# A three-layer transformer on one core: the order of four groups of TensorE work, one moved DMA, and score matmuls of half the width

## The reference

```python
def layer(x, c, w):                      # x: (16, 256, 288), c: (16, 288)
    m0, m1, m2, m3, m4, m5 = split(silu(c) @ w.ada + b_ada, 6)
    q, k, v = heads((layer_norm(x) * (1 + m1) + m0) @ w.qkv + b_qkv)
    attn = softmax(q @ k.T / sqrt(18))   # per sequence and head, 256 x 256
    x = x + m2 * ((attn @ v) @ w.out + b_out)
    h = gelu((layer_norm(x) * (1 + m4) + m3) @ w.up + b_up)
    return x + m5 * (h @ w.down + b_down)
```

## Time and profile before

| | |
|---|---|
| median of 3 runs | 2386.28 us (2383.67 to 2392.12) |
| profiled execution | 2383.67 us, its span 2381.7 us |
| PE busy | 2171.7 us, 91% of the span |
| PEld busy | 1880.9 us, 79% |
| DVE busy | 1382.9 us, 58% |
| ACT busy | 1055.5 us, 44% |
| POOL busy | 993.1 us, 42% |

### The profile page before, as it was taken

The page is one execution under the profiler, slowest core; times in us unless marked ns, Lnnn a source line. Parts: engine busy times, 40 slices in busy tenths (PEclk is TensorE's granted clock), DMA queues, the critical chain, the costliest instruction groups (busy, mean ns, idle before and its releaser), DMA issues. The chain is left out here.

```text
span 2381.7 us, 51475 instructions
## 1 busy us (share of the span) xinstructions
PE 2171.7 (91%) x16443; PEld 1880.9 (79%) x16443; DVE 1382.9 (58%) x3142; ACT 1055.5 (44%) x1859; POOL 993.1 (42%) x988
## 2 busy tenths in 40 slices
PE   6988874789999999898999999998989999999996
PEld 2767653688888888787888888887878888988886
DVE  5378625465656565765656565657556565656551
ACT  2011121445454545454454545453544545454542
POOL 0000002454545454456545454544565454545444
PEclk9755696899999999999999999999999999999998
DMA  8000042433332323234332323332442333332320
GB/s 200 10 2 0 25 150 81 118 95 96 82 99 80 100 78 102 78 106 127 90 101 78 102 81 99 85 98 72 117 118 74 97 85 98 87 97 83 97 72 23
DMA packets 139306, 207.42 MB, mean 87 GB/s; under 512 B 35771, under 2 KB 95835, under 8 KB 138919
## 3 DMA queue, kind: packets, MB, share of 16 engines
q1 hardware_dynamic: 111576, 164.00, 25.3%
q10 hardware_dynamic: 24192, 27.94, 4.3%
q0 software_dynamic: 3456, 14.43, 2.1%
HBM read 99.74 MB, written 20.82 MB: 51 GB/s over the span
## 5 line engine op out<-in xcount | busy, mean ns | idle before, releaser
L1679 DVE TENSOR_REDUCE maxima<-scores 128x4 f32<-128x1024 f32 x384 | 452.4, 1220 | 189.2 <-PE scores L1434 188.6
L1022 POOL TENSOR_TENSOR hidden<-g_full,hidden 128x512 fp32r<-128x512 f32 (+1 forms) x240 | 280.9, 1188 | 347.9 <-ACT hidden L1256 347.6
L1213 ACT ACTIVATE probs<-scores 128x1024 f32<-128x1024 f32 x384 | 383.2, 1026 | 72.9 <-PE pv_ps L1471 47.2
L1496 PEld LDWEIGHTS mlp_ps<-h_mlp,w_up 128*128 128x128 f32 (+1 forms) x3024 | 363.9, 191 | 59.8 <-ACT hidden L1256 34.0
L1496 PE MATMUL mlp_ps<-h_mlp,w_up 128*128 128x256 f32 (+1 forms) x3024 | 384.7, 285 | 28.6 <-ACT hidden L1256 23.2
L1352 PE MATMUL mlp_ps<-w_down,hidden 128*128 128x288 f32 x2592 | 392.0, 296 | 0.0
L1352 PEld LDWEIGHTS mlp_ps<-w_down,hidden 128*128 128x128 f32 x2592 | 373.0, 190 | 21.1
L1434 PE MATMUL scores<-k_stack,q_stack 108*128 108x512 f32 x768 | 252.3, 422 | 40.0 <-DVE maxima L1679 24.0
L1203 ACT ACTIVATE neg_max<-att_ps 16x256 fp32r<-16x256 f32 x48 | 18.0, 374 | 530.3 <-PE att_ps L1444 530.3
L1457 PE MATMUL scores<-q_stack,k_stack 110*128 110x256 f32 x1536 | 246.1, 292 | 4.5 <-ACT probs L1213 3.2
L1457 PEld LDWEIGHTS scores<-q_stack,k_stack 110*128 110x128 f32 x1536 | 206.2, 189 | 34.3 <-issue 19.8
(11 more groups left out here) (171 smaller groups left out, 3412.6 us busy)
## 6 DMA issues: line engine op xcount, KB each, us to landing
q_stack<-qk SPq DMA_DIRECT2D x144, 180.0 KB
k_stack<-qk SPq DMA_DIRECT2D x288, 90.0 KB
inv_sum<-inv_scratch ACTq DMA_DIRECT2D x192, 128.0 KB, 2.8
k_stack<-qk SPq DMA_DIRECT2D x288, 54.0 KB
x_in<-out_x SPq DMA_DIRECT2D x48, 288.0 KB, 3.9
x_mid<-out_x SPq DMA_DIRECT2D x48, 288.0 KB, 4.2
out_x<-x_out SPq DMA_DIRECT2D x48, 288.0 KB, 3.1
q_stack<-qk SPq DMA_DIRECT2D x144, 72.0 KB
```

The costliest lines, as they stand in the source:

```text
L1022: tt(out, full, high.bitcast(F32), ALU.subtract).then_inc(signal, 1)
L1213: evict(probs[:, u % 4, :, :, :], scores[u % 2][:, :, :, :], ACT.Exp, scale=SCALE)\
L1496: last = mm(up_bank[n % 2][:, (m % 2) * T:(m % 2 + 1) * T], w[:, m * P:(m + 1) * P], h, start=count == 0, stop=count == 6)
L1679: nc.vector.tensor_reduce(out=maxima[:, :, :, u], in_=scores[u % 2][:, :, :, :], axis=AX.X, op=ALU.max).then_inc(s_max, 1)
```

## The change

- `negated_maxima`, `negate_maxima`: both DMAs of negated maxima are now sent by SyncE, one after the other; ScalarE sends none and no longer waits for its own eviction.
- `score_unit`: a unit's scores are made by four matmuls of 256 columns (head outside, query tile inside), each with its own weight load, where there were two of 512. The output's index order changes with it, and `unit_max` writes its four results with the two indices exchanged.
- `half_step` of TensorE: `weighted_values` 0 moves ahead of the MLP transposes and of shifted unit 4; shifted unit 5 moves ahead of `weighted_values` 1; `up` 1 moves behind `values` 1, and on ScalarE `gelu` 1 moves behind `v_evict` 1.
- In the score phase each part of `down` comes ahead of its score unit.

```diff
--- before.py
+++ after.py
@@ -956,10 +956,11 @@
                         head_into_stack(j, par, K_PARTS[j], slice(2, 5), 2 * PAIR + HD * par, slice(5, 8), s_stack_b)
 
             def negated_maxima(it):
-
                 hold(s_neg, it + 1 + PRE)
-                sp.dma_start(q_stack[PAIR_ROWS:PAIR_ROWS + 1, :, :].bitcast(F32),
-                             neg_max[0:H // 2, :].bitcast(F32)).then_inc(s_neg_st, 16)
+                for par in range(2):
+                    row = PAIR_ROWS + par
+                    sp.dma_start(q_stack[row:row + 1, :, :].bitcast(F32),
+                                 neg_max[par * 8:par * 8 + 8, :].bitcast(F32)).then_inc(s_neg_st, 16)
 
             def store(it, b):
                 hold(s_x_out, 2 * it + 2 + PRE2)
@@ -1201,9 +1202,6 @@
                 act.wait_ge(s_max_ps, it + 1 + PRE)
                 act.wait_ge(s_neg_st, 32 * it + 16)
                 evict(neg_max[:, :], att_ps[0:H, 0:T], ACT.Copy, scale=-1.0).then_inc(s_neg, 1)
-                act.wait_ge(s_neg, it + 1 + PRE)
-                act.dma_start(q_stack[PAIR_ROWS + 1:PAIR_ROWS + 2, :, :].bitcast(F32),
-                              neg_max[H // 2:H, :].bitcast(F32)).then_inc(s_neg_st, 16)
 
             def exponentials(it, u):
                 act.wait_ge(s_st, 8 * it + u + 1 + PRE)
@@ -1302,12 +1300,10 @@
                     load_table(ACT.Gelu_apprx_tanh)
                     gelu(it - 1, 0)
                 load_sums(it)
-                if before:
-                    gelu(it - 1, 1)
                 if after:
                     v_evict(it + 1, 1)
                 if before:
-                    for n in range(2, UP_USES):
+                    for n in range(1, UP_USES):
                         gelu(it - 1, n)
                         if n == 2:
                             store_inverse(it)
@@ -1430,9 +1426,10 @@
                 else:
                     pe.wait_ge(s_max, 8 * it + u - 1)
                 r = slice(0, PAIR_ROWS)
-                for qt in range(2):
-                    last = mm(scores[u % 2][:, qt, :, :], q_stack[r, u, qt * P:(qt + 1) * P],
-                              k_stack[r, u, :, :], start=True, stop=True)
+                for par in range(2):
+                    for qt in range(2):
+                        last = mm(scores[u % 2][:, par, qt, :], q_stack[r, u, qt * P:(qt + 1) * P],
+                                  k_stack[r, u, par, :], start=True, stop=True)
                 last.then_inc(s_score, 1)
 
             def maxima_transposes(it, after):
@@ -1543,12 +1540,12 @@
                         qk_tiles(it + 1, n, m_between=before)
                     shifted_unit(it, n)
                 shifted_unit(it, 3)
+                weighted_values(it, 0)
                 if before:
                     mlp_transposes(it - 1, after)
                 shifted_unit(it, 4)
-                weighted_values(it, 0)
+                shifted_unit(it, 5)
                 weighted_values(it, 1)
-                shifted_unit(it, 5)
                 shifted_unit(it, 6)
                 if after:
                     values(it + 1, 0)
@@ -1561,11 +1558,10 @@
                     if at(b, 1):
                         pe.wait_ge(s_w_low, converted(OF["w_up"][2], l))
                     up(m, 0)
-                    up(m, 1)
                 if after:
                     values(it + 1, 1)
                 if before:
-                    for n in range(2, UP_USES):
+                    for n in range(1, UP_USES):
                         if at(b, 1) and n == 2:
                             weights_ready("w_up", l)
                         up(m, n)
@@ -1577,10 +1573,10 @@
                 if at(b, 1):
                     weights_ready("w_down", l)
                 for n in range(6):
+                    if before:
+                        down(m, n // 3, n % 3)
                     if after:
                         score_unit(it + 1, n + 2)
-                    if before:
-                        down(m, n // 3, n % 3)
 
             def epilogue():
                 it = L * B - 1
@@ -1676,7 +1672,7 @@
                 if u == 0:
 
                     dve.wait_ge(s_max_ps, it + PRE)
-                nc.vector.tensor_reduce(out=maxima[:, :, :, u], in_=scores[u % 2][:, :, :, :],
+                nc.vector.tensor_reduce(out=maxima[:, :, :, u].rearrange("p q r -> p r q"), in_=scores[u % 2][:, :, :, :],
                                         axis=AX.X, op=ALU.max).then_inc(s_max, 1)
 
             def inverse(it):
```

## The result

The changed kernel takes 2419.38 us (median of 4 runs, 2416.54 to 2432.57), against 2389.2 us for the kernel before in 4 runs of the same session (2383.67 to 2401.7). The ratio is 1.0134, with a 95% interval of 1.0101 to 1.0167. It is slower by 1.3%, clear of 1 by its interval, as forecast; 2421 was predicted. The profiled execution took 2419.03 us, its span 2417.1.

What follows compares the result with a forecast made beforehand. TensorE is 91% busy, but VectorE's chain was taken to set the half step's end; terms 0.3 - 0.3 + 0.13 + 0.65 + 0.03 = +0.8 us, times 38 = 30.4, plus 4.8 for odd ones, gave 2421 us (range 2388 to 2440).

Steps and rivals of the forecast that it cites:

- The forecast's case: Whole program: slower, 2421 us, with VectorE setting the end of the half step; chance 0.77.
- VectorE's chain: Score phase: score unit 2, maximum 2, `normalise`, GpSimd 5.4 us, the `attention_high` cast, maxima 6 and 7, then transposes.
- D: Score phase, `down` ahead of score units: unit 2 0.96 us later, maximum 2 and `normalise` 0.65 later; +0.65 us.
- plain half step: 38 of 47 intervals between maxima transposes, alike, 39.25 us in the one read; predicted +0.8 us each, 30.4 in all.
- A: Both negated-maxima DMAs on SyncE: the second lands late for shifted unit 0; +0.3 us, bounds 0.1 and 0.6.
- B: Weighted values 0 and shifted unit 5 moved earlier: exponential 7 starts sooner, a gain of 0.3 us, bounds 0 and 0.53.
- C: `values` 1 ahead of `up` 1: new wait of some 0.3 us, `up` 2 loses its wait; net +0.13.
- E: Score matmuls of 256 columns instead of 512: extra weight loads hide; +0.03 us, bounds 0 and 0.1.
- rival 3: Score units: added weight loads are exposed, 3.2 us per half step, so 2536 us; chance 0.03.
- odd half steps: The 9 intervals between maxima transposes that are not plain, estimated without rows; together +4.8 us.
- Rival 1: Score phase: TensorE is the bound and VectorE's lateness is hidden; faster, -0.5 us per half step, 2367 us; chance 0.12.
- Rival 2: Whole program: no change, the DMA move hidden and `down` first half hidden; 2386 us; chance 0.08.

## Why the prediction was right, and where it was not

The forecast's case held: VectorE's chain sets the end of the half step, and D makes it longer. Its signs came too: 4.07 us from the first maximum to `normalise` (about 4.1 forecast); `values` 1 waits for `v_sb`, 1227.34 - 1225.39 - 1.69 = 0.26 us; weighted values 2 and 3 together take 1225.39 - 1223.20 = 2.19 us instead of the 1.87 of two groups without a wait, so 0.32 is left of the 0.53. TensorE's idle time at the end is 0.92 us, a little under the 1 us named. The terms, in us per plain half step:

| part | predicted | alone | in the changed kernel |
|---|---|---|---|
| A | +0.3 (0.1 to 0.6) | +0.25 | |
| B | -0.3 (-0.53 to 0) | +0.18 | -0.29 (not run: 0.74 less the other four alone) |
| C | +0.13 (-0.15 to +0.4) | +0.09 | |
| D | +0.65 (0 to 0.95) | +0.66 | +0.21 (undone) |
| E | +0.03 (0 to 0.1) | +0.03 | |
| sum | +0.81 | +1.21 | +0.74 |

The last column's entries for B and D do not add up with each other: B's counts D at its full 0.66, D's is what its removal gives back.

- **A** was read well. The second DMA is issued at about 1209.94 + 0.70 = 1210.64 and shifted unit 0 starts at 1212.67, so issue to use is 2.0 us: the nearer bound, of the earlier trace rows, and not the 2.31 of the earlier trace rows (by which the second DMA would be 1150.68 + 0.70 + 2.31 - 1153.25 = 0.44 us late, not the 0.47 of the text). The restart of the stream adds 0.1. The Trainium skill (DMA: Bandwidth & Descriptors, Issuing engines are not separate DMA queues) says that issuing from several engines saves only the sequencer's time, which is usually small beside the transfer. The trace agrees about what is saved, 0.70 us of issuing. Here that was enough to become a wait in 45 half steps.
- **B** gave 0.37 us at `up` 0 when alone, a little more than the 0.3 taken. In the changed kernel the gain cancels A's 0.27 up to `up` 0. Its cost was missing from the sum: shifted unit 4 releases SyncE's copies, and their last six come 1.2 us later (0.7 to 0.9 with B alone). I named this in the last sentence as a surprise and did not price it. The trace before had the rows for it: unit 5 needs copies whose issue ends at 1174.94 + 4.91 = 1179.85, and it starts at 1149.70 + 32.26 = 1181.96. In the changed kernel the price is zero only because D delays unit 5 by 0.95 us. So the -0.3 came true by D's doing, and with D undone it would not have.
- **C** made its wait of 0.3; the net was 0.08 to 0.09 instead of 0.13.
- **D** was right to 0.01 us as an edit of the kernel before, and so was its path: unit 2, maximum 2, `normalise`, GpSimd, the cast, maxima 6 and 7. The Trainium skill (SBUF — State Buffer, section on the two separate sides) has the later of VectorE and GpSimd blocked for the whole of the other's instruction. The traces agree: the cast ends 0.15 us behind GpSimd's low parts, and in the two runs that only moved it away from them 1.18 and 1.40 us became 0.28.
- **E** was nothing to speak of. The rule on row groups that the prediction cites from the Trainium skill (TensorE: Matmul & The Clock Gate, section The mechanism) does not hold for these matmuls: rival 3 priced exposed loads at 3.2 us per half step, and 0.03 were measured. The same section also lets a load be pulled ahead when it goes to the background weight buffer, and this is the case that the measurement fits.

The sum of the parts measured alone is 1.21 us, far above the 0.74 measured together. Without D the parts do add up: 0.25 + 0.18 + 0.09 + 0.03 = 0.55, and the changed kernel with D undone is 0.53 above before. D and the late copies then overlap: each delays the same last part of the half step, and the longer one counts. The forecast's sum is near the measured one because its two omissions, the copies' delay and this overlap, cancel; in that much it was lucky. Nor does the cast's path carry the whole: with the cast out of the way on both sides 0.36 us of the 0.74 stay.

**The whole program.** 38 half steps gave 29.7 us where 30.4 were forecast. The estimates for the odd half steps failed: +4.8 was taken, -1.9 came. The two with b = 14 changed by -2.5 together (taken: -1.0), the three with b = 1 by +1.0 (+3.6), the two with b = 0 by +0.9 (+1.6), the first and the last by -1.4 (+0.6). Each of these half steps scatters by 1.1 us or more over the 14 profiles (b = 1 of the second layer by 4.0 us, 49.6 to 53.5), so these differences are no measure of the change, and what sets them was not tried. On the profiled execution, forecast +35 and measured +35.4 agree by luck: the setup's +9.1, which is not the change's, stands in for the error of the odd half steps and of the stretch behind the last transposes. On the medians the forecast of 2421 is 2 us off, but as a difference it was +34.7 (from 2386.28) against +30.2 measured (from 2389.2), with the setup's scatter of 16 us in both.

Rival 1 (TensorE as the bound) falls with the run that changed VectorE's order alone and won 0.34 us. Rival 2 falls with the ratio, rival 3 with E alone.

## What to carry to other kernels

Where several chains end close together, price an edit by each: ask of every moved step whom it releases, its queue of DMAs included, and how much slack the one it releases has. Parts measured alone add up only while they delay different things; an edit that seems free may be free because another one is slow. An operation of VectorE that takes long only because it starts under GpSimd's work, as the cast does, is worth moving behind work that others wait for before any other order is tried: here that edit gained 0.34 us per half step, while the five parts together lost 0.74.

## What the runs showed that was not expected

- The cast of 96x256 in `attention_high` takes 0.28 us alone. Where it starts under GpSimd's low parts it takes 0.67 (B alone) to 1.40 us (before) in a kernel's median, and ends 0.15 us behind them. The time shown for such an instruction is mostly a wait.
- SyncE needs 0.70 us to issue a DMA of 8 KB and 4.91 us for six key copies, so a queue of 24 copies has its last landing decided by when it starts. Its slack here was about 0.5 us: 1.2 us of delay became 0.69 at score unit 5.
- The setup code ran at a granted clock of 0.73 to 1.00 between 290 and 320 us, and ended between 402.2 and 418.5 us. Mostly the lower clock went with the later end (0.97: 407.0; 0.78: 416.1), though one kernel with 0.90 was the latest. Why the clock differs there was not tried.
